# Smoothing stage of a graph network kernel: the second rest of every chunk is made by GpSimd instead of VectorE, from each pass's fifth pair of rows on

## The reference

```python
deg = segment_sum(w, dst); dinv = rsqrt(deg); norm = dinv[src] * w * dinv[dst]   # with self loops of weight 1
hh = x
for _ in range(3):
    lx = x - segment_sum(norm[:, None] * x[src], dst)
    y = x - lx                                  # gamma * 2 * (1 - 0.1) is 1
    x = hh + proximal(y - hh)                   # row norm, max(norm - gamma * 0.1, 0) / norm, times the row
```

## Time and profile before

| | |
|---|---|
| median of 3 runs | 8149.56 us (8144.39 to 8155.41) |
| the profiled execution | 8145.88 us |
| its span, first to last instruction | 8144.0 us |
| smoothing, first to last second rest | 4536.7 to 6246.0 us |
| VectorE busy in the loop of pass 0 | 350.9 of 371.8 us |
| GpSimd busy there | 0 |

### The profile page before, as it was taken

How to read it: one execution, slowest core, us unless ns; L and a number is a source line. 1 busy time by engine, 2 the same in 40 slices (tenths; PEclk the granted TensorE clock), 3 DMA queues, 4 the chain that set the end, 5 groups by cost and what they waited for, 6 DMA issues and landing times. The chain is left out here.

```text
span 8144.0 us, 280276 instructions
## 1 busy us (share of the span) xinstructions
PE 6943.6 (85%) x98699; PEld 5906.3 (73%) x98724; DVE 5918.6 (73%) x17405; ACT 4418.0 (54%) x13288; POOL 2861.5 (35%) x2957
## 2 busy tenths in 40 slices
PE   0289999999999989999996588788896899998887
PEld 0155555555555579999996588788896888897877
DVE  1266666666666679899896799799899666676556
ACT  0222222222222269999996587687796565665545
POOL 0068888888888855455454000000000000000000
PEclk9999999999999999999998799999998999998889
DMA  9222232222322247767665688787895666664545
GB/s 383 113 55 61 59 61 59 60 59 60 60 60 61 59 157 231 230 227 230 226 228 174 231 300 292 276 298 283 291 332 205 201 197 197 197 192 137 171 134 157
DMA packets 656410, 1425.57 MB, mean 175 GB/s; under 512 B 284336, under 2 KB 351662, under 8 KB 652737
## 3 DMA queue, kind: packets, MB, share of 16 engines
q1 hardware_dynamic: 538370, 1220.03, 46.6%
q0 software_dynamic: 101792, 92.82, 5.5%
q10 hardware_dynamic: 15700, 105.61, 3.2%
HBM read 982.95 MB, written 433.34 MB: 174 GB/s over the span
## 5 line engine op out<-in xcount | busy, mean ns | idle before, releaser
L243 POOL DMA_INDIRECT sorted_rows<-sort_rows,sort_row_at x1600 | 1975.2, 1234 | 518.0 <-issue 496.4
L1560 ACT ACTIVATE smooth_msg<-smooth_ps_a,smooth_w_rows 128x64 f32<-128x64 f32 x6000 | 1311.6, 333 | 313.3 <-PE smooth_ps_a L1646 297.1
L273 ACT ACTIVATE sort_count<-sort_ps_c 50x50 bf16<-50x50 f32 x1600 | 331.9, 207 | 1983.8 <-PE sort_ps_c L305 1348.2
L1341 ACT ACTIVATE poly_cast<-poly_mat 128x1536 bf16<-128x1536 uint8 x500 | 714.2, 1475 | 462.3 <-PE poly_ps L1362 362.8
L301 PEld LDWEIGHTS sort_ps_r<-sort_count,sort_hot_dt 50*125 50x125 bf16 x1600 | 283.3, 177 | 836.5 <-issue 639.1
L315 PE MATMUL sort_ps_m<-sort_w,sort_hidden 128*125 128x64 f32 x3200 | 879.3, 430 | 0.0
L1668 PE MATMUL smooth_ps_s<-smooth_msg,smooth_hot 128*128 128x64 bf16 x7500 | 769.1, 194 | 76.8 <-DVE smooth_last_part L1799 67.0
L294 PE MATMUL sort_ps_h<-sort_attrs,sort_w 24*128 24x500 f32 x800 | 812.6, 1117 | 2.5 <-DMA sort_attrs<-in_attr_t 2.5
L1668 PE MATMUL smooth_ps_s<-smooth_last_part,smooth_hot 128*128 128x64 bf16 x7500 | 763.6, 194 | 15.9 <-issue 15.9
L1668 PE MATMUL smooth_ps_s<-smooth_rest,smooth_hot 128*128 128x64 bf16 x7500 | 764.7, 194 | 14.3 <-issue 14.3
L1668 PEld LDWEIGHTS smooth_ps_s<-smooth_msg,smooth_hot 128*128 128x128 bf16 x7500 | 685.8, 99 | 111.9 <-DVE smooth_last_part L1799 68.9
(11 more groups left out here) (332 smaller groups left out, 16487.0 us busy)
## 6 DMA issues: line engine op xcount, KB each, us to landing
poly_mat<-counts_t SPq DMA_DIRECT2D x500, 400.0 KB
smooth_src<-src_rows SPq DMA_DIRECT2D x150, 960.0 KB, 5.0
smooth_hot<-hot_rows SPq DMA_DIRECT2D x150, 960.0 KB, 6.9
smooth_src<-src_rows SPq DMA_DIRECT2D x150, 640.0 KB, 6.0
smooth_hot<-hot_rows SPq DMA_DIRECT2D x150, 640.0 KB, 6.3
sorted_rows<-zeros ACTq DMA_DIRECT2D x100, 875.0 KB, 13.3
graph_edges<-sorted_rows SPq DMA_DIRECT2D x125, 700.0 KB
hot_rows<-graph_hot SPq DMA_DIRECT2D x125, 640.0 KB, 3.4
```

Of the source, the lines that this page charges most:

```text
L243: pool.indirect_dma_start(out=sorted_rows, out_offset=bass.IndirectOffsetOnAxis(row_at[u][:, j:j + 1], 0), in_=rows[u][:, j, :], in_offset ...
L1341: act.activation(cast[u][h][:, DVE_S:HR, :], mat[u][h][:, DVE_S:HR, :], ACT.Copy)\
L1560: last = act.activation(at[:, i, :], ps_a[g % 2][:, i * D:(i + 1) * D], ACT.Copy, scale=w_rows[u][:, c * CHUNK + i:c * CHUNK + i + 1])
```

## The change

GpSimd gets a loop over pairs 4 to 24 of each pass. In it, for each of ten chunks, it waits for the first rest (`firsts`) and makes the second rest with the same operands, then raises a new semaphore `pool_rests`. VectorE no longer makes the second rest in these pairs (its condition holds for pairs 0 to 3 alone, see under the diff). TensorE waits for `pool_rests` instead of `rests` in front of the sums of these chunks; its loop now begins at pair 5, with pair 4 written out ahead of it.

```diff
@@ gpsimd
+                def split(k, p, u, c):
+                    pool.wait_ge(firsts, N_CHUNKS * row_of(k, p, u) + c + 1)
+                    pool.sem_inc(taken, 1)
+                    pool.tensor_tensor(last_part[c][:], rest[c][:], high(rest[c]), ALU.subtract).then_inc(pool_rests, 1)
...
                 for k in range(PASSES):
                     spilled.on_pool(pool, k, n, y_sb)
                     pool.wait_ge(spilled.y_in, 16 * k + 16)
                     if k < PASSES - 1:
                         spilled.clear(pool, False)
+                    with pool.Fori(LATE, PAIRS) as p:
+                        for u in two:
+                            for c in range(N_CHUNKS):
+                                split(k, p, u, c)
@@ tensor, add_up
-                    pe.wait_ge(rests, number + 1)
+                    if not isinstance(p, int) or p >= LATE:
+                        pe.wait_ge(pool_rests, number + 1 - N_CHUNKS * 2 * LATE * (k + 1))
+                    else:
+                        pe.wait_ge(rests, number + 1 - N_CHUNKS * (NB - 2 * LATE) * k)
@@ tensor, the passes
-                    with pe.Fori(LATE, PAIRS) as p:
+
+                    pair(k, LATE)
+                    with pe.Fori(LATE + 1, PAIRS) as p:
                         pair(k, p)
@@ vector, pair
                             beside.go(at_once)
-                            dve.wait_ge(firsts, number + 1)
-                            dve.tensor_tensor(last_part[c][:], rest[c][:], high(rest[c]), ALU.subtract)\
-                               .then_inc(rests, 1)
+                            if isinstance(p, int) and p < LATE:
+                                dve.wait_ge(firsts, number + 1)
+                                dve.tensor_tensor(last_part[c][:], rest[c][:], high(rest[c]), ALU.subtract)\
+                                   .then_inc(rests, 1)
                             beside.go(at_once)
```

More of the change, by code:

```diff
@@ L1504, in smooth @@
         step, normed, rooted, posted, taken = (sem(n) for n in ("step", "normed", "rooted", "posted", "taken"))
-        first = sem("first")
+        first, pool_rests = sem("first"), sem("pool_rests")
         row_of = lambda k, p, u: k * NB + u + 2 * p
```

## The result

The changed kernel takes 8318.76 us (median of 4 runs, 8313.05 to 8321.97) against 8150.18 us before: a ratio of 1.0207, 95% interval 1.0194 to 1.0220, so 169 us slower. The prediction was 8447 us, within a range of 8230 to 8640. The sign and the mechanism were right, and the loss was put too high by a factor of 1.8.

The account below looks back on a forecast made before the run. VectorE was taken as the bound. Blocked chunks plus steps added 161, 90, 27 and 15 us over the stretches and 8 for pair 4: +301 us on 8145.9 gives 8447 us, range 8230 to 8640.

Parts of the forecast that it names:

- What bounds the kernel: In the smoothing, VectorE sets the pace at 21.87 us a pair; TensorE would come next at 18.3 us.
- That the two engines block each other: First rest and GpSimd's second rest exclude each other in SBUF; the first rest ends 0.68 us behind GpSimd, 2.23 us a chunk.
- The duration on GpSimd: A second rest of 640 elements on GpSimd takes 1.45 us, estimated from 622 ns for 260 elements.
- The hand-over: GpSimd starts 0.10 us after the first rest ends: 0.08 from the trace, 0.02 for the register instruction.
- The steps come on top: Steps of post on VectorE find no free time beside GpSimd: 3.84 us a pair, 2.39 in pass 2, plus links.
- side by side: Rival: the first rest does not stand for GpSimd; a pair takes 18.5 us, the program about 7950; chance 0.12.
- The short instruction: Rival: engines block, but GpSimd's second rest needs only about 0.98 us; program about 8150; chance 0.08.
- TensorE's clock: Granted clock in the loop at 0.8 to 0.95; rival: it stays at 1.2 GHz, program about 8700, chance 0.06.
- Costed at nothing: TensorE's written-out pair 4 and other wait, GpSimd's loop register work, and the later last_part were given no cost.

Follow-up runs that it names:

- e3: Changed kernel, but from pair 4 on nobody makes the second rest and TensorE waits for the first rest: 7954.56 us, ratio 0.9757.
- e1: Changed kernel, but from pair 4 on the first rest reads one operand from a PSUM tile of zeros: 8130.9 us, ratio 0.9972.
- e2: Changed kernel, but GpSimd sets two SBUF tiles to zero per chunk and nobody makes the second rest: 7999.91 us, ratio 0.9817.
- e4: Changed kernel, but GpSimd's second rest covers 512 of 640 columns and nobody makes the other 128: 8188.33 us, ratio 1.0045.
- e5: Changed kernel without the register instruction between GpSimd's wait for the first rest and its subtraction: 8363.66 us, ratio 1.0259.
- e8: Kernel before, with two steps of post given to ScalarE in the loops of passes 0 and 1, chain one chunk earlier: 8128.68 us, ratio 0.9975.

## Why the prediction was right, and what was off

**What bounds the kernel:** right. VectorE set the pace, and e3 shows that with less work on it TensorE is next, at 18.05 us a pair (18.3 predicted).

**That the two engines block each other:** right, and shown by e1 (one operand in PSUM, and no first rest stands), e2 and e4. The price of a blocked rest was read from one short instruction of the graph stage and held for another of 640 columns in float32: in the changed kernel the first rest took over 0.9 us in 281 cases and ended 0.68 us behind GpSimd's end in each, as worked out.

**The duration on GpSimd:** mis-sized. It was put at 1.45 us by proportion from 260 columns; it took 1.25, on the mean 1.28 with its own waiting. The two lengths measured, in e4 and in the changed kernel, give a line (an estimate from two points): 512 columns 1.04 us, 640 columns 1.25, so 1.66 ns a column and 0.19 us fixed. The 622 ns of the earlier trace rows lie on it, so proportion was wrong in spreading a third of those 622 ns over the columns. (1.45 - 1.28) x 630 = 107 us too much. The trace held a hint in the CAST of 228 ns, which I used for the lower bound only.

**The hand-over:** 0.18 us instead of 0.10. The register instruction was put at 0.02 us; e5 shows that it costs 0.10. That is 0.08 x 630 = 50 us too little.

**The steps come on top:** the step of the argument that failed in part. It said that whichever engine is let in first, the other waits, so that every step adds its length. But the step right behind the scaling starts 0.06 us before GpSimd and passes, and with that it lies in a gap that was already counted. And two kinds with one tensor input never wait: TENSOR_REDUCE lies wholly beside GpSimd's instruction, and RECIPROCAL passes even when GpSimd is first (e5). The sum had 301 us; less 107, plus 50, it is 244, and the stage grew by some 170. The 74 us that are left over 63 pairs are 1.2 us a pair. An estimate from the rows comes near that: the first steps of seven chunks, with their links, are 1.8 us and the TENSOR_REDUCE 0.3; against that, behind a step that stood the first rest runs in full, 0.82 and not 0.68 us, in six chunks, 0.8 us. e5, where most first steps no longer slip in, costs 49 us more although its hand-over is shorter by 0.10 us.

The forecast came out nearer than its terms: two were too high, by 107 and 74 us, and one was too low by 50, so that a part of the error cancelled by luck.

**The rivals:** side by side did not come about, and its price (7950) is confirmed by e3 as that of a kernel in which the second rests cost nothing (7954.56). The short instruction did not come about either, though 1.25 us lies near the lower bound. The point from which it decides was put at 0.98 us; by e4, 1.04 us still loses 36 us, 0.06 us for each of 630 chunks, so an estimate from e4 gives 0.98 as well. That it fits is partly luck, since the hand-over and the steps behind it were both off.

**TensorE's clock:** wrong as a sign, without a price. The granted clock was to fall to 0.8 to 0.95 in the loop. It stayed at 0.99 and 1.00 there, with TensorE busy for 84% of it; it was 0.94 in pairs 22 to 24 of pass 0, as before. It played no part.

**Costed at nothing:** fine where it can be seen. TensorE waited for the second rest in each row, but its waits followed VectorE's and GpSimd's pace. For pair 4 the sum had 8 us; it took 4.6 us less than before. The pairs behind the spilled edges differ from run to run by some microseconds in all kernels, so neither number means much, and no run tests that term.

## What to carry to other kernels

Before an element-wise instruction goes to GpSimd, ask not whether GpSimd has time, but what VectorE will do meanwhile. If that reads two SBUF tensors, the two take turns, and one pays GpSimd's slower rate (1.25 us here for what VectorE does in 0.74) plus a hand-over. With one operand in PSUM it ran beside GpSimd at its usual length (0.82 us, e1). ScalarE's scaling was as long in the changed kernel as before (median 330 against 332 ns), and work moved to ScalarE gave back about what it was worth once it was ready when ScalarE came to it (e8). A rise in an engine's busy time with less work on it is the sign to look for.

## What the runs showed that was not expected

- A register instruction between a wait and its GpSimd instruction costs 0.10 us (0.18 against 0.08 us from the end of the awaited instruction to the start). Taking it away made the kernel 49 us slower, because GpSimd then came before VectorE's next small step in six chunks of ten.
- A GpSimd instruction that only writes (a memset) leaves VectorE's instructions with two SBUF inputs alone, 0.29 us for L1777, but holds up TENSOR_SCALAR (0.16 to 0.69 us) and CAST (0.22 to 0.75 us).
- RECIPROCAL and TENSOR_REDUCE on SBUF do not stand for GpSimd, though they too have one tensor in and one out: 0.15 us for L1755 of e5, which starts 0.04 us behind GpSimd, and 0.29 us for L1749 of e1, which starts 0.25 us behind it.
